# Cross-attention over four layers: two of the eight key tiles of P V in three fp16 products, with the output projection later in the slot and a new order of the first slot

## The reference, cut to what matters

```python
# x: (4, 512, 256); ctx: (4, 1024, 512); four layers, each of them x = layer(x, ctx)
# layers 0, 2, 3: 16 heads of 64
q, k, v = x @ Wq, ctx @ Wk, ctx @ Wv
logits = einsum('bhqd,bhkd->bhqk', q, k) * 64 ** -0.5
logits[:, :, :, token_indices_A] += -20 * (1 - mask_A)[:, None]      # by query row
logits[:, :, :, token_indices_B] += -20 * (1 - mask_B)[:, None]
x = einsum('bhqk,bhkd->bhqd', softmax(logits), v) reshaped @ Wo + bo + x
# layer 1: x is RMS-normed first; 16 query heads of 16 share 4 key/value heads
```

## Time and profile before

| what | us |
| --- | --- |
| median of 3 runs | 3499.44 (3497.91 to 3499.72) |
| the profiled execution's own time | 3498.58 |
| its span, first to last instruction | 3496.4 |
| PE busy in the span | 3364.5 |
| DVE, POOL, ACT busy | 2350.3, 2183.0, 1766.3 |
| mean granted TensorE clock | 0.993 of full speed |

### The profile page before, as it was taken

One profiled execution on the slowest core, in us unless ns is written; L12 is line 12 of the kernel. 1 busy time (PEld: TensorE's weight loads), 2 busy tenths in 40 slices (PEclk: granted clock), 3 DMA queues, 4 the chain that ended last, 5 costly groups with the idle time before them and its releaser, 6 DMA issues.

```text
span 3496.4 us, 70163 instructions
## 1 busy us (share of the span) xinstructions
PE 3364.5 (96%) x27442; PEld 1544.6 (44%) x27442; DVE 2350.3 (67%) x4444; ACT 1766.3 (51%) x2230; POOL 2183.0 (62%) x1050
## 2 busy tenths in 40 slices
PE   6999999999997888889999999999999999999998
PEld 3444444444442322234444444444444444444443
DVE  5666666666656788856676666666666666666666
ACT  4444444444445677764444444444444444444444
POOL 4877777777650000028777777777787677767776
PEclk8999999999999999999999999999999999999999
DMA  4000000000000000000000000000000000000000
GB/s 145 10 10 10 1 10 10 9 3 9 6 10 11 8 12 17 17 1 10 10 1 10 10 10 1 10 10 9 3 10 10 1 10 10 10 1 10 3 1 25
DMA packets 50178, 42.10 MB, mean 12 GB/s; under 512 B 4928, under 2 KB 42176, under 8 KB 49856
## 3 DMA queue, kind: packets, MB, share of 16 engines
q1 hardware_dynamic: 49136, 37.08, 3.5%
q10 hardware_dynamic: 720, 0.53, 0.1%
HBM read 32.36 MB, written 2.10 MB: 10 GB/s over the span
## 4 chain that ended last, share of the span: by engine, by line
PE 90%; ACT 3%; DVE 3%; POOL 2%; issue 2%; DMA 0%; SPq 0%; ACTq 0%; POOLq 0%; DVEq 0%
PE ps_j L863 39%; PE ps_j L1052 19%; PE ps_st L1012 13%; PE ps_sm L946 6%; PE ps_st L997 3%; PE ps_j L1039 3%; ACT pt L1473 2%; PE ps_sm L1026 2%; POOL acc L719 2%; PE ps_j L1072 1%; PE ps_st L946 1%; PE ps_j L955 1%; PE ps_j L1088 0%; PE ps_j L1063 0%; DVE nmg L1893 0%
## 5 line engine op out<-in xcount | busy, mean ns | idle before, releaser
L719 POOL TENSOR_TENSOR acc<-acc,pt 128x1024 f32<-128x1024 f32 x570 | 1365.3, 2395 | 438.9 <-ACT pt L1473 384.8
L1473 ACT ACTIVATE pt<-ps_st 128x1024 f32<-128x1024 f32 x768 | 743.0, 1019 | 447.0 <-PE ps_st L1012 435.2
L1052 PE MATMUL ps_j<-pt,v 128*64 128x512 f32 x3040 | 694.2, 598 | 1.4 <-DVE q_l L1808 1.3
L1903 DVE CUSTOM_DVE_ANT_0 ps_sm<-ps_sm,bias_m,nmx 128x512 f32<-128x512 f32 x666 | 480.3, 757 | 272.6 <-PE ps_j L946 227.6
L863 PE MATMUL ps_j<-w_h,ctx_h 128*128 128x128 f16 x3072 | 532.6, 220 | 1.6 <-ACT rinv L1489 1.1
L863 PE MATMUL ps_j<-w_l,ctx_h 128*128 128x128 f16 x3072 | 531.5, 219 | 0.0
L863 PE MATMUL ps_j<-w_h,ctx_l 128*128 128x128 f16 x3072 | 531.4, 219 | 0.0
L1903 DVE CUSTOM_DVE_ANT_0 ps_sm<-ps_sm,bias_m 128x512 f32<-128x512 f32 x486 | 334.5, 706 | 197.1 <-PE ps_j L946 186.4
L740 POOL TENSOR_TENSOR o_un<-o_un,rinv 128x512 f32<-128x512 f32 x111 | 142.0, 1280 | 477.2 <-ACT rinv L1485 294.9
L1052 PEld LDWEIGHTS ps_j<-pt,v 128*64 128x64 f32 x3040 | 201.7, 136 | 407.6 <-issue 369.6
L1940 DVE RECIPROCAL rinv<-rinv 128x256 f32<-128x256 f32 x190 | 331.3, 1746 | 14.0 <-ACT rinv L1489 4.5
(11 more groups left out here) (186 smaller groups left out, 5483.0 us busy)
## 6 DMA issues: line engine op xcount, KB each, us to landing
w_raw<-wk SPq DMA_DIRECT2D x25, 256.0 KB, 2.7
pt<-ctx_t SPq DMA_DIRECT2D x6, 1024.0 KB, 7.8
w_raw<-wv SPq DMA_DIRECT2D x24, 256.0 KB, 3.7
wo_raw<-wo SPq DMA_DIRECT2D x28, 128.0 KB, 2.0
w_raw<-wq SPq DMA_DIRECT2D x24, 128.0 KB, 2.8
k_h<-k_l SPq DMA_DIRECT2D x72, 32.0 KB, 1.9
x<-x_t SPq DMA_DIRECT2D x4, 512.0 KB, 8.9
acc<-ctx_t SPq DMA_DIRECT2D x2, 1024.0 KB, 8.1
```

What stands on the lines that cost most here:

```text
L719: G.tensor_tensor(total, first, pt[:, n % RING, :], ALU.add).then_inc(s_acc, 1)
L1052: last = MM(dst[h * HD:(h + 1) * HD, :], values_of(p)[:, kt, h * HD:(h + 1) * HD], pt[:, (units(p) + kt) % RING, h * TQ:(h + 1) * TQ], sta ...
L1473: A(pt[:, n % RING, :], src.rearrange("p h q -> p (h q)"), ACT.Exp).then_inc(s_exp, 1)
L1903: last = V.tensor_tensor_reduce(out=src, in0=src, in1=bias_m[:, t, half * HALF:(half + 1) * HALF], scale=-1.0, scalar=nmx[:, 0, t, h:h + 1 ...
```

## The change

Four things are edited.

1. Key tiles 2 and 3 of P V in 88 problems (1 to 27 and 49 to 109, `in_terms`) are multiplied as three fp16 products. The exponential is now written with a bias of ln 1024 in all 96 problems with 64-wide heads; the factor divides out with the row sums. ACT rounds the probabilities (`probs_hi`) and half of V's first bank (`values_hi`), DVE computes the rests (`probs_lo`, `values_lo`). A tile's fp32 form stands two places further in the ring, and its two fp16 parts in its own place.
2. On DVE `probs_lo` of tile 2 comes behind the second reciprocal, and that of tile 3 behind the second K rest; `values_lo` of the next problem stands between the opening and the closing maxima of the third block.
3. `project_out(s - 1, 0)` and its `add_out` go from ahead of `attend(s, 0)` to the slot's end, where both halves now stand together, and the banks of `ps_j` in the second half of a turned slot are dealt anew.
4. Slot -1 gets a form of its own (`lead_slot`), in which maxima and parts of projections alternate; in slot -2 the rest of batch 0's x goes from POOL to DVE ahead of the second context rest, the mask arithmetic goes behind the first Q rest, and one context rest goes from DVE to POOL.

```diff
+def in_terms(p):
+    return p >= 1 and turned(p - 1) and turned(p) and turned(p + 1)
+TERM_TILES = (2, 3)
+def parted(p, kt):
+    return in_terms(p) and kt in TERM_TILES
@@ bank_users, turned slot
             if nxt:
                 then("v0", s + 1, 1)
             opening(2, 0)
+            then("pva", s, 1)
+            opening(3, 0)
+            if nxt:
+                then("v1", s + 1, 1)
+                then("nm0", s + 1, 0)
             if past:
-                then("out0", s - 1, 1)
-            then("pva", s, 0)
-            opening(3, 1)
-            if nxt:
-                then("v1", s + 1, 0)
-                then("nm0", s + 1, 1)
-            if past:
+                then("out0", s - 1, 0)
                 then("out1", s - 1, 1)
@@ where things stand
+        def whole(p, kt):
+            return pt[:, (units(p) + kt + (2 if parted(p, kt) else 0)) % RING, :]
+        def parts(p, kt):
+            both = pt[:, (units(p) + kt) % RING, :].bitcast(F16)
+            return both[:, 0:2 * TQ], both[:, 2 * TQ:4 * TQ]
+        def value_parts(p):
+            both = v32[:, p % 2, 2:4, :].bitcast(F16)
+            return both[:, :, 0:P], both[:, :, P:2 * P]
@@ PE, take
                     elif before in ("v0", "v1"):
                         pe.wait_ge(s_v_sb, values_before(m) + 1 + int(before[1]))
+                        if in_terms(m) and before == "v0":
+                            pe.wait_ge(s_v_l, terms_before(m) + 1)
@@ PE, attend
                     kt = part * 4 + k
+                    if parted(p, kt):
+                        n = terms_before(p)
+                        pe.wait_ge(s_v_l, n + 1)
+                        pe.wait_ge(s_p_l, 2 * n + k - 1)
+                        (vh, vl), (ph, pl) = value_parts(p), parts(p, kt)
+                        for i, (v, q) in enumerate(((vh, ph), (vh, pl), (vl, ph))):
+                            for h in range(2):
+                                last = MM(dst[h * HD:(h + 1) * HD, :], v[:, k - 2, h * HD:(h + 1) * HD],
+                                          q[:, h * TQ:(h + 1) * TQ], start=False, stop=k == 3 and i == 2)
+                        continue
@@ PE, turned_slot
                 score_block(2)
-                if past:
-                    project_out(s - 1, 0)
                 attend(s, 0)
                 score_block(3)
 ...
                 if past:
+                    project_out(s - 1, 0)
                     project_out(s - 1, 1)
@@ ACT
+            def values_hi(p):
+                act.wait_ge(s_v, values_before(p) + 1)
 ...
+                A(value_parts(p)[0], bank("v0", p)[:, 2 * P:4 * P].rearrange("p (k d) -> p k d", k=2), ACT.Copy,
+                  scale=VS / WS)
+            def place_free(n, lent=True):
 ...
+                q, k = owner(n - 2)
+                if lent and not grouped(q) and parted(q, k):
+                    act.wait_ge(s_acc, ADDS * wides(q) + added(k))
+                    act.wait_ge(s_p_l, 2 * terms_before(q) + k - 1)
+            def probs_hi(p, j):
+                act.wait_ge(s_exp, units(p) + j + 1)
+                place_free(units(p) + j)
+                A(parts(p, j)[0], whole(p, j), ACT.Copy).then_inc(s_p_h, 1)
@@ ACT, turned_slot
                 if far:
                     queries_hi(s + 2)
-                    if not splits_x(s):
-                        keys_hi(s + 2, 0)
+                if termed:
+                    probs_hi(s, 2)
+                if far and not splits_x(s):
+                    keys_hi(s + 2, 0)
+                if termed:
+                    probs_hi(s, 3)
+                if far:
                     keys_hi(s + 2, 1)
                 if past:
                     output_hi(s - 1)
+                if nxt and in_terms(s + 1):
+                    values_hi(s + 1)
@@ DVE
+            def values_lo(p):
+                dve.wait_ge(s_v_sb, values_before(p) + 1)
+                hi, lo = value_parts(p)
+                split_lo(lo, bank("v0", p)[:, 2 * P:4 * P].rearrange("p (k d) -> p k d", k=2), VS / WS, hi
+                         ).then_inc(s_v_l, 1)
+            def probs_lo(p, j):
+                dve.wait_ge(s_p_h, 2 * terms_before(p) + j - 1)
+                hi, lo = parts(p, j)
+                V.tensor_tensor(lo, whole(p, j), hi, ALU.subtract).then_inc(s_p_l, 1)
@@ DVE, turned_slot
                 if past and not grouped(s - 1):
                     reciprocal(s - 1, 1)
+                if in_terms(s):
+                    probs_lo(s, 2)
                 if far:
                     keys_lo(s + 2, 1)
-                peak()
-                peak()
-                if past:
-                    add_out(s - 1, 0)
+                if in_terms(s):
+                    probs_lo(s, 3)
+                peak()
+                if nxt and in_terms(s + 1):
+                    values_lo(s + 1)
+                peak()
 ...
                 if past:
+                    add_out(s - 1, 0)
                     add_out(s - 1, 1)
@@ PE, lead_slot (slot -1): nine units of maxima, and between them
+                peak()
+                bias_matrix(2)
+                project_v(0, 0, range(0, 2))
+                peak()
+                bias_matrix(3)
+                project_v(0, 0, range(2, 4))
+                peak()
+                bias_matrix(4)
+                project_k(1, 0, 0)
 ...
```

More of the change, by code:

```diff
@@ L49 @@
 N_CONST, N_EARLY = 4, 5
-FLAG_LO, FLAG_M, FLAG_GQ, FLAG_GK, FLAG_EPS, FLAG_GM = range(6)
+FLAG_LO, FLAG_M, FLAG_GQ, FLAG_GK, FLAG_EPS, FLAG_GM, FLAG_PS = range(7)
+PS = 1024.0
+TERM_TILES = (2, 3)
 ADDS = KT - 1
@@ L175, in splits_x, with terms_before @@
     return p < N and not grouped(p) and p - STARTS[layer_of(p)] < B
+def in_terms(p):
+    return p >= 1 and turned(p - 1) and turned(p) and turned(p + 1)
+def terms_before(p):
+    return sum(in_terms(i) for i in range(p))
+def parted(p, kt):
+    return in_terms(p) and kt in TERM_TILES
 def place_of(p, u):
@@ L508, in build @@
         s_done = sem("s_done")
+        s_v_l = sem("s_v_l")
+        s_p_h = sem("s_p_h")
+        s_p_l = sem("s_p_l")
         s_end_add_g = sem("s_end_add_g")
@@ L714, in add @@
                         pool.wait_ge(s_pv, KT * (groups(p) + p - G1 - 1))
-                    first = pt[:, (n - 1) % RING, :]
+                    first = whole(p, 0)
                 else:
@@ L718, in add @@
                     first = total
-                G.tensor_tensor(total, first, pt[:, n % RING, :], ALU.add).then_inc(s_acc, 1)
+                G.tensor_tensor(total, first, whole(p, kt), ALU.add).then_inc(s_acc, 1)
             def sums_lo(p):
@@ L1118, in score_block @@
                     peak()
-                    if s == -1 and i < 3:
-                        bias_matrix(2 * i + 2)
                     if now:
@@ L1123, in score_block @@
                     peak()
-                    if s == -1 and i < 3:
-                        bias_matrix(2 * i + 3)
                 score_block(0)
@@ L1177, in wide_slot, with lead_slot, peak @@
                     bias_matrix(1)
+            def lead_slot():
+                units_here = iter([unit for place in passes(-1) for unit in place])
+                def peak():
+                    maxima(*next(units_here))
+                peak()
[8 more added lines that the diff above has]
+                peak()
+                bias_matrix(5)
+                project_k(1, 0, 1)
+                peak()
+                bias_matrix(6)
+                project_k(1, 1, 0)
+                peak()
+                bias_matrix(7)
+                peak()
+                project_k(1, 1, 1)
+                peak()
+                project_q(1, 0)
+                project_v(0, 1, range(0, 2))
+                rows_of_maxima(0, 0)
+                project_v(0, 1, range(2, 4))
+                peak()
             def turned_slot(s):
@@ L1572, in context @@
                         context_hi(n)
-                def bias(*parts):
-                    for n in parts:
-                        bias_out(n)
                 if grouped(s - 1):
@@ L1621, in wide_slot @@
                     context(3)
-                elif s == -1:
-                    context(6, 7)
                 if now:
@@ L1646, in wide_slot, with lead_slot @@
                     act.wait_ge(s_init, 1)
-                    bias(0, 1)
+                    bias_out(0)
+                    bias_out(1)
+                    split_x_hi(1)
                 if now and s % B == 0:
                     wo_hi(set_of(s))
+            def lead_slot():
+                for n in (2, 3):
+                    bias_out(n)
+                values(0, 0)
+                bias_out(4)
+                context_hi(4)
+                bias_out(5)
+                keys_hi(1, 0)
+                bias_out(6)
+                context_hi(5)
+                bias_out(7)
+                keys_hi(1, 1)
+                context_hi(6)
+                columns_of_maxima(0)
+                queries_hi(1)
+                values(0, 1)
```

(29 more changed lines are left out.)

118 lines of the change are left out of this document (62 added, 56 removed).

## The result

| | before | after |
| --- | --- | --- |
| median | 3498.7 us (4 runs) | 3543.4 us (4 runs, 3539.7 to 3544.8) |
| ratio, 95% interval | 1 | 1.0127 (1.0114 to 1.0139) |
| the profiled execution's own time | 3498.58 | 3539.71 |
| its span | 3496.4 | 3537.8 |

A forecast was written before the change was run, and what follows sets the result against it. PE, without idle time in turned slots, was taken to bound the kernel. From 3498.6 us, turned slots add 54.6 and the lead takes 11: 3542.2, so 3543 (60%, 3525 to 3560); whole range 3498 to 3572.

The forecast's parts named there:

- split slots: Six turned slots (1, 49, 78 to 81) where POOL also splits x and is late: 1.47 us each, +8.8.
- the lead: Stretch ahead of slot 0: its first product at about 51 instead of 64.81; -11 us, bounds -3 and -20.
- What PE saves: P V's two fp16 tiles save 0.44 us a slot; adjoining output halves save a shape change, 0.10.
- What P V waits for: P V of tiles 0 to 3 takes V's bank, held until `values_lo` ends: 0.47 us late with DVE on time.
- DVE is not on time: Second `probs_lo` stands until POOL's normalization ends; third block's opening maxima start 0.31 us late, P V 0.78 in all.
- the 1.8 among the prediction's signs: Expected in the changed profile: the second `probs_lo` on DVE about 1.8 us long instead of 1.2.
- The rival without a collision: DVE's subtractions don't collide with POOL, opening maxima on time: slot +0.23 us, 3510 with the lead; 15%.
- The rival in which POOL goes first: POOL's normalization takes the ports before the first subtraction; opening maxima 0.84 us later, 3617 us; 7%.
- The second output half: It takes the second V half's bank and waits for ACT's copy: 0.30 us in each of 91 slots.
- The rival on it: ACT's copy of the second V half is in time for the output half: -27 us, 3516; 10%.
- The other side: V's bank is free when PE comes, and PE's 0.54 us are kept in 91 slots: 3440 us; 8%.
- What hides: ACT's two copies, 1.06 us each, stand in gaps where ACT waits for PE's K, so they hide.

The follow-up runs named there:

- the output alone: New first slots plus the output projection's new place and banks, all P V in fp32, no bias, against new first slots alone (3487.7 us): 3501.0 us.
- the last three runs: Changed kernel with V's parts in their own place, old output order: 3466.4 us without bias; 3476.2 with; 3454.4 without bias, six x-splitting problems in fp32.

## Why the prediction came out right

Its mechanism held and so did nearly every size; one term was missing (+0.14 a slot), and two that were taken 0.10 too large together covered most of it. That the sum came out so close is in part luck: the missing term is worth 12 us, the two too large ones 9, the split slots came 2 us cheaper than forecast, and the executions of the changed kernel alone spread over 5 us.

| step, us | predicted | measured |
| --- | --- | --- |
| two tiles in fp16 | -0.44 | -0.42 |
| one shape change less | -0.10 | -0.10 (by the slot of the output alone) |
| P V waits for `values_lo`, opening maxima on time | +0.47 | +0.43 (P's rests out) |
| the same, through the collision | +0.31 | +0.25 |
| second output half waits for ACT | +0.30 | +0.29 |
| slower exponential | not seen | +0.14 |
| an ordinary turned slot | +0.54 | +0.58 |
| the lead | -11 | -12.7 up to the row sums of slot 1, in an execution with a higher clock; -10.8 alone, by the medians |

- *What PE saves.* P V takes 3.17 us where 3.15 was worked out, so the change from fp32 to fp16 within a shape costs 0.02 at most.
- *What P V waits for.* `values_lo` takes 0.41 instead of 0.46, and so the wait is 0.67 instead of 0.78. That the wait hangs on it alone is shown: without V's rests it is gone.
- *DVE is not on time.* The collision ran instruction by instruction as written (1.16, 2.12 and 1.69 us, where 1.22, 2.18 and 1.67 follow from the chain; the 1.8 among the prediction's signs does not). The rival without a collision would have had POOL at 1.27; the run without P's rests has that, and its slot is 0.245 shorter. The rival in which POOL goes first did not occur: POOL starts 0.16 behind DVE. By the port rule cited in the prediction (the Trainium skill, "SBUF — State Buffer", section "Who interferes with whom"), the trace agrees in both orders of issue.
- *The second output half.* The wait is 0.29, with release 0.15 behind ACT's end, the one that no row of before showed. The rival on it falls. Its net price with the shape change, 0.19 a slot, is the run of the output alone.
- *The other side* (no waits, 3440) falls as it stood, but its premise, that PE's gain is real, is what the last three runs use.
- *What hides: the failed step.* ACT's two additional copies do hide. But the exponential was passed over: its bias costs 89 to 90 ns, and "ACT is busy 887.6 of 1864 us" was read as room. At one place there is next to none: K's first product takes the bank of the row sums, and without the bias ACT's copy releases it only 0.04 us before PE comes. Taking the bias out gives back 15 us by the medians (10.7 by the profiled executions). The price could have been looked up: the Trainium skill ("ScalarE: Activation LUTs", section "What ACT_TABLE_LOAD costs") gives about 93 ns for each operand that is a pointer to one value a partition; by that figure the trace agrees, at 89.
- *Split slots.* The six were to cost 1.47 each, 8.8 together; they cost 6.8. The rows called slot 78 in the earlier trace rows are those of the next one, 79; the first split slot has the same order before, additions to 2489.44 and the second reciprocal to 2488.88. After the change P V is as late in slot 78 as elsewhere (0.63 printed), and POOL ends its additions there at 2510.92, ahead of the second reciprocal's end at 2511.39. The moved output half does this: with the lead alone the additions end 0.56 behind the reciprocal, with the output moved as well 0.38 ahead of it. The 0.94 between them is one output half more on PE (0.65) and its wait (0.29), ahead of the row sums. The prediction took the reciprocal's place in the slot as unchanged. What the six cost above an ordinary slot appears later, as waits of up to 1.11 ahead of maxima.
- *Sum.* In the profiled execution: 79 ordinary distances by 0.58 = 45.6, the others 8.4, the lead -12.7, together +41.3 and measured +41.1 (3539.7; 3542.2 was predicted). The median of the runs lies 3.7 above that execution; its mean granted clock was 0.996, that of the other three 0.994. The prediction has no term for the clock.

## What to carry to other kernels

Fewer products on the engine that bounds the kernel are worth what they save only if no bank that it takes next hangs on a new result; before adding a split, look up who holds the input's bank and for how much longer. Give the new operands a place of their own, even if that means an additional copy: together with the output projection back in its old place this turned +1.3% into -0.6% with the same arithmetic, and into -0.9% without the bias. Leaving out the slots in which the helper engine has no pause made it -1.25%. A small addition to an instruction off the critical path counts almost in full where the bounding engine waits for something right behind it; look for the bank or buffer that hangs on it, a busy share says nothing on that. And compare the granted clock of two executions before a gain in a stretch with idle time is put down to the new order.

## What the runs showed of the hardware

- ACT's exponential of 128 x 1024 fp32 from PSUM takes 1109 ns with a per-partition bias from SBUF and 1020 without, in 768 of each.
- A DVE subtraction of two SBUF operands and POOL's multiplication of two such exclude each other, and the later one takes nearly its whole length behind the end of the first: DVE's 1024 elements take 1.16 alone and end 1.08 behind POOL's end (2421.65 and 2420.57), POOL's 512 take 1.27 alone and end 1.12 behind DVE's. The K rest on DVE between them, which reads one operand from PSUM, runs its 0.68 beside POOL. POOL's subtraction of 256 elements takes 0.67 when nothing is in its way.
- A tile of P V (two heads, 512 columns each) takes 0.87 us in fp32 and 0.66 in three fp16 products: from the first fp32 product at 2423.39 to the first in fp16 at 2425.13 it is 1.74 for two tiles, from there to 2426.56 it is 1.43 for two, 0.10 of it the shape change.
- In the slot where PE waited 2.58 us for POOL, the granted clock of TensorE was 0.50 for 6.8 us, from 0.9 ahead of the wait's end on; where it waited 1.98 for DVE, it was 0.50 for 3.4 us, from 0.8 behind the wait's end on (V's parts in their own place, without and with the bias).
